# All gathers of embedding rows issued in GpSimd's opening, none between its products

## What is computed

```python
# tokens: x (2, 1024)
base = emb_table[token_ids]; dom = domain_map[token_ids]
out = base
for d in range(8):
    mask = (dom == d)[..., None]
    out = out + 0.1 * (base @ W_exp[d].T @ W_proj[d].T) * mask
h = out
# attention with a state for each head, one step for each token
q, k, v = split(layernorm(h) @ Wqkv_w.T + Wqkv_b);  k = k / 4
state = retention * state + Gamma * outer(v_t, k_t)      # 16 x 16 for each head
y_t   = (W_static + state) @ q_t
h = h + y @ out_w.T + out_b
# per-token and per-channel quantized product
x = layernorm(h); x_q, s = round(x / s); w_q, sw = round(w / sw)
h = h + (x_q @ w_q.T) * s * sw + bias
```

## Time and profile before

| | |
|---|---|
| runs of the kernel before | 253.32, 252.12 and 250.42 us, median 252.12 |
| the profiled execution | 251.63 us, of which the traced span is 249.8 us |
| mean granted PE clock in it | 0.972 of full speed |
| PE, DVE, POOL, ACT busy | 222.4, 195.7, 190.4, 108.0 us |
| DMA | 21.24 MB, mean 85 GB/s |

### The profile page before, as it was taken

One profiled execution on the slowest core, in us unless ns is written; L12 is line 12 of the kernel. 1 busy time (PEld: TensorE's weight loads), 2 busy tenths in 40 slices (PEclk: granted clock), 3 DMA queues, 4 the chain that ended last, 5 costly groups with the idle time before them and its releaser, 6 DMA issues.

```text
span 249.8 us, 7732 instructions
## 1 busy us (share of the span) xinstructions
PE 222.4 (89%) x3218; PEld 163.5 (65%) x3218; DVE 195.7 (78%) x389; ACT 108.0 (43%) x272; POOL 190.4 (76%) x100
## 2 busy tenths in 40 slices
PE   3999976998899999999989999999886995788971
PEld 3989543775467686776847767768465683566860
DVE  0158794598956897898799977996989989999493
ACT  5405665036332313697931136978300247510150
POOL 5970049999999999998599997764999999652032
PEclk9999999999999999999999999999998899599997
DMA  5593126411144821101540440016414400020002
GB/s 155 138 254 133 42 87 192 149 45 42 38 129 87 272 72 46 45 1 45 179 145 21 104 152 3 0 46 175 134 35 99 155 3 4 1 87 3 0 0 84
DMA packets 19442, 21.24 MB, mean 85 GB/s; under 512 B 2416, under 2 KB 13904, under 8 KB 19408
## 3 DMA queue, kind: packets, MB, share of 16 engines
q1 hardware_dynamic: 18640, 18.65, 24.7%
q0 software_dynamic: 768, 2.11, 3.5%
HBM read 14.98 MB, written 5.77 MB: 83 GB/s over the span
## 4 chain that ended last, share of the span: by engine, by line
PE 69%; DVE 15%; issue 5%; ACT 4%; DMA 3%; POOL 3%; SPq 0%; DVEq 0%; ACTq 0%; POOLq 0%
PE y_ps L1157 10%; PE scr L1005 10%; PE w_ps L1137 9%; PE scr L982 6%; PE y_ps L1099 5%; PE scr L995 5%; PE scr L1019 5%; PE scr L1034 4%; PE scr L959 4%; DVE zz L923 3%; POOL uu L473 3%; PE scr L1072 2%; PE scr L1058 2%; PE y_ps L1148 2%; PE y_ps L1043 2%
## 5 line engine op out<-in xcount | busy, mean ns | idle before, releaser
L473 POOL TENSOR_TENSOR uu<-vg,kk 128x1024 f32<-128x1024 f32 x64 | 151.3, 2405 | 28.3 <-DMA vg<-v_far 19.1
L923 DVE TENSOR_TENSOR zz<-e_hg,q_ps 128x1524 f32<-128x1524 f32 x31 | 53.6, 1728 | 0.0
L892 DVE TENSOR_TENSOR_SCAN e_hg<-decay,w_ps 128x512 f32<-128x512 f32 x32 | 38.9, 1217 | 10.4 <-PE w_ps L1137 9.8
L1137 PE MATMUL w_ps<-uu,comb 128*32 128x128 f32 x1024 | 36.7, 284 | 1.4 <-POOL uu L473 1.1
L1157 PE MATMUL y_ps<-zz,coll 128*32 128x128 f32 x768 | 28.9, 284 | 6.3 <-DVE zz L923 6.3
L1137 PEld LDWEIGHTS w_ps<-uu,comb 128*32 128x32 f32 x1024 | 28.8, 114 | 8.6 <-issue 7.4
L1157 PEld LDWEIGHTS y_ps<-zz,coll 128*32 128x32 f32 x768 | 20.4, 112 | 20.3 <-issue 9.5
L553 ACT ACTIVATE junk<-tok_dom 128x256 bf16<-128x256 f32 x24 | 9.7, 407 | 28.6 <-DVE tok_dom L690 28.6
L909 DVE TENSOR_TENSOR zz<-e_hg,q_ps 128x512 f32<-128x512 f32 x32 | 21.7, 678 | 0.0
L401 POOL DMA_INDIRECT tok_dom<-in_table,ids_sb x16 | 15.5, 969 | 6.2 <-issue 3.5
L415 POOL TENSOR_TENSOR tok_dom<-tok_dom,bf 128x1024 f32<-128x1024 f32 (+1 forms) x5 | 9.0, 1791 | 13.7 <-ACT tmp_b L578 11.8
(11 more groups left out here) (126 smaller groups left out, 373.6 us busy)
## 6 DMA issues: line engine op xcount, KB each, us to landing
vg<-v_far SPq DMA_DIRECT2D x32, 256.0 KB, 4.2
v_far<-v_sb SPq DMA_DIRECT2D x8, 256.0 KB, 3.8
out_h<-tok_dom SPq DMA_DIRECT2D x8, 256.0 KB, 2.3
k_far<-kk SPq DMA_DIRECT2D x12, 128.0 KB
k_sb<-k_far SPq DMA_DIRECT2D x4, 384.0 KB, 3.4
wexp<-in_w_exp SPq DMA_DIRECT2D x1, 256.0 KB
tok_dom<-in_table,ids_sb POOLq DMA_INDIRECT x16, 4.3
wproj<-in_w_proj SPq DMA_DIRECT2D x1, 256.0 KB
```

The source lines that it names most:

```text
L473: pool.tensor_tensor(uu[:, g % NU, two], v_of.to_broadcast(shape), k_of.to_broadcast(shape), ALU.mult).then_inc(s_u, 1)
L892: dve.tensor_tensor_scan(states(g).rearrange("p a m -> p (a m)"), decay[:, NA * n:NA * (n + 1)].rearrange("p a m -> p (a m)"), w.rearrange ...
L923: dve.tensor_tensor(z, e.to_broadcast(shape), q.to_broadcast(shape), ALU.mult).then_inc(s_z, 1)
L1137: last = pe.matmul(w_ps[32 * hp:32 * hp + 32, g % NW, a], comb[:, NA * n + a, hp], uu[:, g % NU, hp, a], start=True, stop=True, skip_group ...
```

## The change

POOL's calendar alone is changed. All twelve gathers of chunks 1 to 3 are now issued in slot -1, in the order of the tokens, right behind `decays`. Nothing is issued between POOL's products any more until the bias at slot 67. The entry `after 0.1` at slot 19 is dropped, and so its wait. Instructions, tiles and the other engines' calendars stay.

```diff
 POOL_CALENDAR = """
-    -1: gathers 0.1, gathers 0.0, decays 0.0, gathers 2.0, gathers 1.0, gathers 1.1; 19: after 0.1; 24: gathers 2.1;
-    26: gathers 3.0; 30: gathers 3.1; 67: bias 0.0; 74: out 0.0, out 0.1; 99: bias 1.0; 106: out 1.0, out 1.1; 127:
-    bias 2.0, out 2.0, out 2.1, assist 3.0, bias 3.0, bias 3.1, out 3.0
+    -1: gathers 0.1, gathers 0.0, decays 0.0, gathers 1.0, gathers 1.1, gathers 2.0, gathers 2.1, gathers 3.0, gathers
+    3.1; 67: bias 0.0; 74: out 0.0, out 0.1; 99: bias 1.0; 106: out 1.0, out 1.1; 127: bias 2.0, out 2.0, out 2.1,
+    assist 3.0, bias 3.0, bias 3.1, out 3.0
 """
```

## The result

The changed kernel took 255.94 us (median of 4 runs, 255.08 to 257.98) against 251.87 us for the kernel before on the same chip (4 runs, 250.42 to 253.32). The ratio is 1.0173, with a 95% interval of 1.0125 to 1.0220. It is slower, though whether by 2% stays open, and outside the range that was given. The profiled execution is the fastest of the four, 255.08 us with a span of 253.0 us; before it was 251.63 and 249.8. So the traces have to account for +3.2 us, and the medians say some +4.

The account below looks back on a forecast made before the run. PE, busy throughout between 61 and 125 us, was taken as the bound, POOL having slack. Terms -2.3 + 0.1 + 0.1 = -2.1 gave 249.5 us from the profiled 251.63, or 250.0 us from the median 252.12; range 247.4 to 253.5.

Parts of the forecast that it names:

- Six gathers leave the middle: Between POOL's products: 7.5 us of gathers go, but only lengthen POOL's waits for `vg` or PE; taken as 0.
- PE's stops beside the gathers: K stage at 66.14 and combine at 80.30: stops of 1.55 and 0.78 us go if gathers cause them; 2.3 us gained.
- I count no loss at it: DVE, next to be late once PE's stops go, had itself waited for PE and moves with it; no loss counted.
- Rival 1: PE's two stops are its own, a hitch in instruction supply; gathers only fill POOL's slack: 252.1 us, chance 0.20.
- Six gathers more in the opening: POOL's added gathers run from 18.9 to 26.2 us, before its first product at 34.55; 8.4 us of cover left.
- Traffic: Added gathers getting in front of the weights DVE needs at 23.20, or meeting the first v's write: 0.1 us for both.
- DVE beside the added gathers: From 22.7 to 26.2 us gathers might hold DVE's small operations and `comb`: 0.1 us taken, bounds 0 and 2.85.
- the lock of rows 5: DVE instructions with two SBUF inputs and POOL ones reading SBUF exclude each other, as at the first product: 3.98 and 2.46 us.
- A delay of DVE in the opening is paid one for one: The first combine, for which PE waits, hangs on the end of DVE's chain, so any DVE delay there counts fully.
- Rival 2: The stops move: landing data stops PE's first k stage at 27.8, one stop of 1.55 us: 251.5 us, chance 0.10.
- Rival 3: Three gathers between 22.7 and 26.2 hold DVE, first product 2.85 us later: 255.0 us with stops, 252.7 without; chance 0.16.
- rival 4: Removing PE's idle time before the combine at 193 us ends its low clock: another 1.7 us, 248.3 us, chance 0.12.

Follow-up runs that it names:

- c1_spare: Kernel before plus six spare gathers in the opening, into memory nobody reads yet, the middle keeping its own gathers: 256.94 us, ratio 1.0239.
- l2_pause: Changed kernel with POOL pausing before its last six gathers until the first `xhat`, at about 21.4 us: 248.44 us, ratio 0.9944.
- d1_one_pair: Kernel before with one pair of gathers (2.1) moved into the opening and `after 0.1` dropped: ratio 0.9898.
- d2_two_pairs: Kernel before with two pairs of gathers (2.1 and 3.0) moved into the opening: ratio 1.0035.
- t1_sp_loads: Changed kernel with its last six gathers replaced by plain loads of as many bytes that SP issues in the opening: 248.38 us, ratio 0.9878.
- b1_wide: Kernel before with gathers 2.1 in the opening, 3.0 at slot 46 and 3.1 at slot 58, beside PE's wide matmuls: ratio 0.9961.
- b3_slots: Kernel before with its opening left, gathers 2.1 at slot 26, 3.0 at 46, 3.1 at 58, beside PE's wide matmuls: ratio 0.9927.
- its second run: The changed kernel once more, with nothing altered, measured against the kernel before: 255.73 us, ratio 1.0175.
- w0_no_wakes: Changed kernel without all 27 idle matmuls of PE between `corr 0.1` and `v 0.0`: ratio 1.0043.
- p1_pool_plain: Changed kernel with its last six gathers issued by POOL as plain DMAs of consecutive rows: ratio 0.9978.
- l1_late_six: Changed kernel with POOL waiting before its last six gathers for the second `xhat_t` of chunk 0, at 25.8 us: 266.2 us.
- r_after: Changed kernel with `decays` moved behind the first ten gathers: 255.4 us, ratio 1.0113.

## Why the prediction was wrong

*Six gathers leave the middle, 0 by itself*: right. POOL's waits for `vg` went from 19.1 to 22.6 us and for PE from 9.1 to 11.4, 5.8 us more for the 7 forecast.

*PE's stops beside the gathers, -2.3*: right in cause, a little too large. The k stage takes 1.77 us, 1.53 less. At the combine of group 7 only 0.3 of 0.78 is left over, since the matmul behind it now waits 0.43 us for DVE. "I count no loss at it" was the error there. c1_spare, where the gathers stay and the stop with them, shows the cause. Rival 1 is out.

*Six gathers more in the opening, "so 8.4 us of cover is left"*: this is the step that failed. Every number of it came true, the starts, the 0.95 us, the end at 26.2. But it asks only who waits for POOL. I had just read two rows in which PE stops while POOL gathers, had priced them at 2.3 us for the place that the gathers leave, and had not asked what PE does at the place that they go to. In its place the runs showed +8.3 us at the first v: about 6.1 us of stop (the third transpose of chunk 0 starts at 28.53 instead of about 22.4) and 2.2 us for the instructions behind it at half clock.

*Traffic, +0.1*: right for the changed kernel, whose DVE does not wait for the weights; the loads of the same size that SP issued cost 0.16 us there. It isn't always so small: in l2_pause that wait was 2.24 us, above the 0.4 to 0.8 that the prediction had as the most the gathers can put in front. What delayed the weights there is open.

*DVE beside the added gathers, +0.1, at most 2.85*: the lock of rows 5 was not it. `comb` came at 29.30 instead of 25.13 but took its 4.43 us unchanged: it was late because PE's signal was. "A delay of DVE in the opening is paid one for one" holds where DVE's chain is the last to end: from the start of `comb` to the first combine it is 16.03 us before, and 16.03 to 16.05 in d1_one_pair, d2_two_pairs, t1_sp_loads, b1_wide and b3_slots, with `comb` anywhere from 25.26 to 30.63. So the 5.5 us of d2 in the front came through DVE. In the changed kernel it is 18.71: there the first product waited for v, and the 4.2 us of `comb` cost nothing more. That the first product would shorten (3.98 to 2.61 us) I hadn't counted; it gave 1.4.

*The rivals.* Rival 2, "the stops move", named the mechanism and had 0.10. Its place (27.8) and its price (one stop, 1.55 us) were wrong. Its cause, the data rather than the issuing, isn't refuted: the stretch ended 2.0 to 2.7 us behind the last gather issued before it, and 0.5 to 1.2 us behind the last packet of those (changed kernel, its second run, c1_spare, d2_two_pairs; in the second run the last gather, which `comb` held until 30.24, is left out). In the middle a pair of gathers stops PE for 0.8 to 1.6 us; a row of twelve costs the front five times that. Rival 3, the slower one, is out, though its 255.0 us lies near the result and its two signs, `comb` later than 25.13 and the first combine behind 42, both came. That is luck: no DVE operation of the opening took longer, and a late signal of PE gives the same signs. The gain of rival 4 came, but not by its mechanism: the combine at 197.27 runs at full clock in 1.06 us, and 1.6 us are gained, yet PE idles 1.82 us ahead of that stretch in both kernels. What decides its clock is open.

Together, from the execution traced: +8.3 - 1.4 - 2.0 - 1.6 = +3.3, against +3.2 in the spans.

What stays open is what is held. That PE gets on at 0.7 us per instruction and that its signals rise 2.4 to 6.2 us behind the matmuls would fit one jam on PE's way to its instructions and semaphores, with the gathers in the same way; no record shows that way itself. The one block of instructions fetched in the front (16 KB, queue q8 of the page) is not late: it starts at 19.9 us in the changed kernel and at 20.1 before, and takes 1.0 us in both. Nor did a run separate the issuing from the transfers, or indirect from plain DMAs in a row as long.

One rival stands untested, the profiler itself. The traces lose records where PE's signals are late. Sixteen gathers end in 256 landing events; the trace holds 44 of them in the changed kernel, 71 in its second run, 165 before, but all 256 in b1_wide, l2_pause and w0_no_wakes, and all 160 of ten gathers in p1_pool_plain. These four are the traces in which no signal of PE is late. A jam in writing the records would look the same as one in the program. Every execution of the sets above comes with a span and a granted clock, so each was taken with the profiler, and no run shows what the row of gathers costs without it.

## What to carry to other kernels

POOL's slack says what gathers cost POOL, not what they cost PE: a long unbroken row of indirect DMAs beside a dense stream of small PE instructions stopped PE for 6 us here, as far as profiled executions tell, and the clock then took 2 more. Read PE's "issue" gaps beside every group of gathers, and when you move gathers, look at what PE will run beside their new place. Here rows of six to eight gathers with the rest beside wide matmuls, or twelve with a break in them, came out 0.4 to 1.0% faster than the kernel before.

## What was not expected of the hardware

- PE's one-by-one stretches have a fixed step: starts 1.40, 1.36 and 1.44 us apart in the changed kernel, 1.39 in its second run, 1.41 with ten gathers, 1.44 and 2.09 in c1_spare. Each is two or three times 0.70 us within 0.04.
- DVE's `comb` holds a gather. A gather takes 0.95 us, but 4.30 (l1_late_six, at 25.87), 4.79 (l2_pause, at 27.77) and 5.01 us (r_after, at 25.23) where it meets `comb`, which itself keeps its 4.43. The Trainium skill ("SBUF — State Buffer", section "Who interferes with whom") infers that a `tensor_tensor` does not keep GpSimd from generating descriptors. In these three rows one with two SBUF inputs did hold a gather, and the measurement decides. A gather also reads its token numbers (`ids_sb`) from SBUF, though, and the rows don't tell whether that read or the descriptors were held.
- In the other direction, back-to-back products on POOL held one small DVE operation for all ten of them, 23.9 us in l1_late_six. The same section of the Trainium skill states that the one which comes second blocks until the other is through; here it did not get its turn between two products either.
